# Layer 3 attention: work placed anew inside the steps of the memory chain, local attention in halves as full products, keys placed and values joined by GpSimd

## The reference, cut to what matters

```python
def step(carry, seg):
    mem, z = carry
    qq, kk, vv = seg
    sigma_q = jax.nn.elu(qq) + 1.0
    scores = jnp.einsum('bhsk,bhtk->bhst', qq, kk) / scale
    scores = jnp.where(causal_mask, scores, -jnp.inf)
    att_dot = jax.nn.softmax(scores, axis=-1) @ vv
    att_mem = sigma_q @ mem / (sigma_q @ z)
    sigma_k = jax.nn.elu(kk) + 1.0
    delta = vv - sigma_k @ mem / (sigma_k @ z)
    mem_new = mem + jnp.einsum('bhsk,bhsv->bhkv', sigma_k, delta)
    z_new = z + sigma_k.sum(axis=-2, keepdims=True).transpose(0, 1, 3, 2)
    att = beta * att_mem + (1.0 - beta) * att_dot
    out = att.reshape(Bsz, SEG, H * DV) @ Wo
    return ((mem_new, z_new), out)
```

## Time and profile before

| | |
|---|---|
| median of 3 runs | 1845.53 us (1842.15 to 1848.94) |
| span of the profiled execution | 1830.4 us |
| TensorE busy, of the span | 1617.1 us (88%) |
| VectorE busy | 984.5 us (54%) |
| ScalarE busy | 820.3 us (45%) |
| GpSimd busy | 355.9 us (19%) |

### The profile page before, as it was taken

How to read it: one execution, slowest core, us unless ns; L and a number is a source line. 1 busy time by engine, 2 the same in 40 slices (tenths; PEclk the granted TensorE clock), 3 DMA queues, 4 the chain that set the end, 5 groups by cost and what they waited for, 6 DMA issues and landing times. The chain is left out here.

```text
span 1830.4 us, 28085 instructions
## 1 busy us (share of the span) xinstructions
PE 1617.1 (88%) x9357; PEld 1274.0 (70%) x9358; DVE 984.5 (54%) x2336; ACT 820.3 (45%) x1798; POOL 355.9 (19%) x372
## 2 busy tenths in 40 slices
PE   4999996997639999787979989989999999999897
PEld 3778654875528888665637767867888888888655
DVE  2367346344555544224474445576676667666476
ACT  3577253333325555105755433364455445544344
POOL 2400020211066666573002121220000000000000
PEclk9999986998759999768989989999999999999899
DMA  3000030142615555332001042220000000000200
GB/s 121 12 18 1 1 147 9 43 105 59 255 60 168 168 170 168 107 104 78 1 0 38 32 117 77 72 81 1 18 17 17 0 17 17 17 0 0 46 0 23
DMA packets 55628, 109.35 MB, mean 60 GB/s; under 512 B 9905, under 2 KB 37425, under 8 KB 53914
## 3 DMA queue, kind: packets, MB, share of 16 engines
q1 hardware_dynamic: 45330, 82.10, 14.0%
q0 software_dynamic: 9168, 25.05, 4.8%
q10 hardware_dynamic: 1040, 1.05, 0.2%
HBM read 89.39 MB, written 18.78 MB: 59 GB/s over the span
## 5 line engine op out<-in xcount | busy, mean ns | idle before, releaser
L2776 ACT ACTIVATE l_mem<-bank 128x129 f32<-128x129 f32 x240 | 64.8, 279 | 185.6 <-PE bank L2630 184.7
L1681 POOL DMA_INDIRECT h_modulated<-l1f_rows,ln_rstd x127 | 120.5, 949 | 77.4 <-PE bank L1748 71.1
L1761 PE MATMUL bank<-l1f_up,l1f_wt 128*128 x508 | 104.4, 329 | 0.0
L2630 PE MATMUL bank<-l_dr,l_nkt 128*128 128x129 f32 x480 | 99.1, 309 | 2.9 <-DVE l_dr L2934 2.0
L3069 POOL MEMSET l3f_imp<- 96x2048 f32 x1 | 1.8, 1807 | 507.2 <-POOLq L88 507.2
L2931 DVE RECIPROCAL l_inv<-bank 128x1 f32<-128x1 f32 x240 | 38.9, 162 | 109.8 <-PE bank L2640 109.0
L2640 PE MATMUL bank<-l_mem,l_sg 128*128 128x129 f32 x480 | 84.4, 294 | 6.0 <-ACT l_mem L2776 0.2
L2934 DVE SCALAR_TENSOR_TENSOR l_dr<-bank,l_inv,l_v 128x128 f32<-128x128 f32 x240 | 84.3, 351 | 8.5
L1775 PE MATMUL bank<-l1f_down,ln_rstd 96*128 x254 | 87.5, 426 | 0.1
L2630 PEld LDWEIGHTS bank<-l_dr,l_nkt 128*128 128x128 f32 x480 | 68.5, 189 | 23.6 <-DVE l_dr L2934 19.4
L1804 PE MATMUL bank<-l1f_wt,ln_square 128*128 128x128 f32 x256 | 68.8, 426 | 18.2 <-DMA ln_square<-l1f_y_rows,l1f_back_at 16.9
(11 more groups left out here) (610 smaller groups left out, 4373.6 us busy)
## 6 DMA issues: line engine op xcount, KB each, us to landing
l1f_y_rows<-h_modulated SPq DMA_DIRECT2D x127, 128.0 KB
l1f_up<-in_l1f_up SPq DMA_DIRECT2D x8, 1536.0 KB
l_w<-in_l_w SPq DMA_DIRECT2D x9, 768.0 KB, 4.2
wmod<-in_wmod SPq DMA_DIRECT2D x4, 1536.0 KB, 10.1
l1f_down<-in_l1f_down SPq DMA_DIRECT2D x4, 1536.0 KB, 21.9
l2e_w<-in_l2f_win SPq DMA_DIRECT2D x14, 256.0 KB, 2.7
l_w<-in_l_wqk SPq DMA_DIRECT2D x8, 256.0 KB, 2.7
l0m_w<-in_l0f_win SPq DMA_DIRECT2D x8, 256.0 KB, 2.7
```

Of the source, the lines that this page charges most:

```text
L1681: pool.indirect_dma_start(xg[:, i % GETS], None, table, bass.IndirectOffsetOnAxis(ap=listing[:, i:i + 1], axis=0)).then_inc(got[i % GETS], 16)
L1761: last = pe.matmul(k.bank[:, UP + i % 2, 0:2 * F], xt[:, i % 2, b], up[:, bass.ds(owner_reg[i], 1), b, :], start=(b == 0), stop=(b == DB - 1))
L2630: pe.matmul(k.bank[:, MEM + a, 0:W1], nkt[:, a, n // 2, n % 2, :], dr[:, a, n, 0:W1], start=False, stop=False, skip_group_check=True).then ...
L2776: act.activation(mem[:, a, (n + 1) % 2, 0:W1], k.bank[:, MEM + a, 0:W1], ACT.Identity).then_inc(s["mem_copied"], 1)
```

## The change

Only `l3_attention` is changed.

1. GpSimd places the keys (`place_keys`), four copies of 128 x 512 a pair, instead of ScalarE. It also joins the values: `vj` has all 128 rows of each tile and head, made by two copies of 64 rows x 2048 elements a pair.
2. Local attention is 8 products of 128 rows and 128 columns a head (`vj` with the whole turned probabilities, whose off-diagonal blocks are zero), in two groups of four in two steps, each waiting for one of the two copies of the probabilities, which ScalarE now makes in two successive steps. `dot_scale` works on these halves.
3. `turn_reads` uses `pe.transpose` in the place of a product for tiles 0 to 6, in steps 14 (head 0) and 15 (head 1), without waits on the deltas; the last tile keeps its product (`turn_last_reads`).
4. The work in a step has three places: before the writes, between the write of head 0 and that of head 1, and after both. The output projection has 5 products in steps 1 to 4 and 4 in steps 5 to 7 (the last two one each in the second and third place).
5. Pieces of VectorE and ScalarE move to other steps accordingly.

```diff
+    OUT_PARTS = (0, 5, 10, 15, 20, 24, 28, 32)
+        vj = sb("vj", [P, TT, HP, P])
 ... on GpSimd:
+                def place_keys(i, a, c):
+                    if a or c:
+                        pool.wait_ge(s["keys_placed"], i * 4 + 2 * a + c)
+                    pool.wait_ge(s["sigma_ready"], i * 8 + 4 * a + c + 1)
+                    pool.tensor_copy(sg[:, a, 4 * c:4 * c + 4, 0::3, :], by_segment(keys[:, a, chunk(c)])
+                                     ).then_inc(s["keys_placed"], 1)
+                for i in range(PAIRS):
...
+                    for a in range(HP):
+                        for c in range(NCH):
+                            place_keys(i, a, c)
+                    pool.wait_ge(s["keys_placed"], i * 4 + 4)
+                    pool.wait_ge(s["v_even_copied"], i * 2 + 2)
+                    pool.tensor_copy(vj[EVEN], v[EVEN, :, :, 0, :]).then_inc(s["v_joined"], 1)
+                    pool.wait_ge(s["v_odd_copied"], i * 2 + 2)
+                    pool.wait_ge(s["v_joined"], i * 2 + 1)
+                    pool.tensor_copy(vj[ODD], v[ODD, :, :, 1, :]).then_inc(s["v_joined"], 1)
 ... on TensorE, turn_reads:
-                            last = pe.matmul(k.bank[:, 2 * a + o, t * S:(t + 1) * S], dr[half, a, 2 * t + o, 0:P],
-                                             turn[half, half], start=True, stop=True)
+                            last = pe.transpose(k.bank[:, 2 * a + o, t * S:(t + 1) * S], dr[half, a, 2 * t + o, 0:P],
+                                                turn[half, half])
 ... read_memory:
+                        if n == NS - 1 and not a:
+                            pe.wait_ge(s["dot_scaled"], i * 4 + 4)
 ... local_attention:
-                        for t in range(TT):
-                            for o, half in enumerate(HALF):
-                                last = pe.matmul(k.bank[:, 2 + o, t * S:(t + 1) * S], v[half, t, a, o, :],
-                                                 pt[half, a, t, half], start=True, stop=True)
+                        if begin % 4 == 0:
+                            pe.wait_ge(s["pt_copied"], i * 4 + (2 * a + c + 1))
...
+                        for t in range(begin, end):
+                            last = pe.matmul(k.bank[:, 2 + c, (t % 4) * P:(t % 4 + 1) * P], vj[:, t, a, :],
+                                             pt[:, a, t, :], start=True, stop=True)
 ... the places in a step:
+                    def before_writes(n):
+                        if n <= 7 and not first:
+                            project_out(i, OUT_PARTS[n - 1], OUT_PARTS[n] - 2)
+                        if n in (8, 11):
+                            turn_probs((n - 8) // 3, 0, 4)
+                        if n in (9, 10):
+                            local_attention(0, 4 * (n - 9), 4 * (n - 9) + 3)
+                        if n in (12, 13):
+                            local_attention(1, 4 * (n - 12), 4 * (n - 12) + 3)
                         if n == 14:
+                            turn_reads(i, 0, 0, LAST)
+                        if n == 15:
+                            turn_reads(i, 1, 0, LAST)
+                    def between_writes(n):
+                        if n <= 7 and not first:
+                            project_out(i, OUT_PARTS[n] - 2, OUT_PARTS[n] - 1)
+                        if n in (8, 11):
+                            turn_probs((n - 8) // 3, 4, 6)
+                        if n in (9, 10):
+                            local_attention(0, 4 * (n - 9) + 3, 4 * (n - 9) + 4)
+                        if n in (12, 13):
+                            local_attention(1, 4 * (n - 12) + 3, 4 * (n - 12) + 4)
+                    def after_writes(n):
+                        if n <= 7 and not first:
+                            project_out(i, OUT_PARTS[n] - 1, OUT_PARTS[n])
+                        if n in (8, 11):
+                            turn_probs((n - 8) // 3, 6, 8)
...
                         if n < NS - 1:
-                            for a in range(HP):
-                                write_memory(n, a)
-                            after_write(n)
+                            write_memory(n, 0)
+                            between_writes(n)
+                            write_memory(n, 1)
+                            after_writes(n)
 ... on ScalarE, behind the memory copies of step n:
-                        if n in (7, 9):
-                            for c in range(NCH):
-                                probs_copy((n - 7) // 2, c)
-                        if n in (8, 11):
-                            dot_scale((n - 8) // 3)
+                        if n in (8, 9):
+                            probs_copy(0, n - 8)
+                        if n in (11, 12):
+                            probs_copy(1, n - 11)
+                        if n in (9, 10):
+                            dot_scale(0, n - 9)
+                        if n in (12, 13):
+                            dot_scale(1, n - 12)
```

More of the change, by code:

```diff
@@ L2554, in turn_reads, with turn_last_reads @@
                 def turn_reads(i, a, begin, end):
-                    if begin == 0:
-                        for o in range(2):
-                            pe.wait_ge(s["dot_scaled" if a else "pt_copied"], i * 4 + (2 + o + 1))
-                    if begin == LAST:
-                        pe.wait_ge(s["reads_added"], i * 8 + (2 * a + 2))
                     for t in range(begin, end):
-                        pe.wait_ge(s["delta_ready"], i * CHAIN + (HP * 2 * t + a + 1))
                         for o, half in enumerate((ODD, EVEN)):
-                            last = pe.matmul(k.bank[:, 2 * a + o, t * S:(t + 1) * S], dr[half, a, 2 * t + o, 0:P],
-                                             turn[half, half], start=True, stop=True)
-                    if end >= LAST:
+                            last = pe.transpose(k.bank[:, 2 * a + o, t * S:(t + 1) * S], dr[half, a, 2 * t + o, 0:P],
+                                                turn[half, half])
+                    if end == LAST:
                         last.then_inc(s["turned"], 1)
+                def turn_last_reads(i, a):
+                    pe.wait_ge(s["reads_added"], i * 8 + (2 * a + 2))
+                    pe.wait_ge(s["delta_ready"], i * CHAIN + (HP * 2 * LAST + a + 1))
+                    for o, half in enumerate((ODD, EVEN)):
+                        last = pe.matmul(k.bank[:, 2 * a + o, LAST * S:TT * S], dr[half, a, 2 * LAST + o, 0:P],
+                                         turn[half, half], start=True, stop=True)
+                    last.then_inc(s["turned"], 1)
                 def pair(i, first):
@@ L2689, in after_write, with local_attention @@
-                    def after_write(n):
-                        if n <= 6 and not first:
-                            project_out(i, 5 * n - 2, 5 * n)
-                        if n == 7:
-                            turn_probs(0, 1)
-                        if n == 9:
-                            turn_probs(1, 1)
+                        if end % 4 == 0:
+                            last.then_inc(s["pt_ready"], 1)
+                    def local_attention(a, begin, end):
+                        c = begin // 4
+                        if begin % 4 == 0:
+                            pe.wait_ge(s["pt_copied"], i * 4 + (2 * a + c + 1))
+                            if a:
+                                pe.wait_ge(s["dot_scaled"], i * 4 + (c + 1))
+                        if begin == 0 and a == 0:
+                            pe.wait_ge(s["v_joined"], i * 2 + 2)
+                            if not first:
+                                pe.wait_ge(s["x_added"], i)
+                        for t in range(begin, end):
+                            last = pe.matmul(k.bank[:, 2 + c, (t % 4) * P:(t % 4 + 1) * P], vj[:, t, a, :],
+                                             pt[:, a, t, :], start=True, stop=True)
+                        if end % 4 == 0:
+                            last.then_inc(s["dot_ready"], 1)
```

97 lines of the change are left out of this document (33 added, 64 removed).

## The result

The changed kernel takes 1810.8 us (median of four runs, 1808.8 to 1812.9) where the kernel before, timed beside it, takes 1845.3: a ratio of 0.982 (95% interval 0.980 to 0.984). It is 34.5 us faster; the forecast was 28 (1817, range 1801 to 1835).

The account below looks back on a forecast made before the run. A chain of read, reciprocal, delta, write and copy was taken as the bound. Steps save 5.6 us a pair, less 0.3 tail and 1.7 GpSimd hold: 3.6, 28 in all, from 1845.5 to 1817 us, range 1801 to 1835.

Parts of the forecast that it names:

- The bound: Each pair's memory chain: read, reciprocal, delta, write, copy sets the time; TensorE's other work costs what it puts before a write.
- steps 2 to 14: Memory-chain steps of a pair after the first, forecast at 2.05, 2.2, 2.3 or 2.47 us each.
- Four full products at 2.47: Steps 9, 10, 12, 13: products wait for one copy of turned probabilities, so each step takes 2.47 us.
- Rival C: Copies of turned probabilities come late on ScalarE; the four steps with products stay near 3.2 us; 1840 us, chance 0.08.
- Local attention "no cheaper" as full products: TensorE's local attention: 8 full products or 32 half records both take 1.78 us a head.
- Turns: Turns of the reads as half-height transposes: 14 records a head at 0.056 us, 0.78 us; bounds 0.056 and 0.109.
- rival B: Half-height transposes on TensorE go at 0.109 us a record; 12 us more, 1829 us, chance 0.15.
- Tail: Between copy 14 and the next pair's projections, head 1's turns come in: 0.3 us a pair lost, bounds 0 and 0.8.
- The hold: GpSimd's placements and joins delay VectorE's SBUF-only sigma and capping before the first reciprocal: 1.7 us a pair, bounds 0 and 6.9.
- rival A: One-operand GpSimd copies hold nothing up on VectorE; 8 x 1.7 us back, 1804 us, chance 0.18.
- Rival D: Joins of 4.51 us hold VectorE between sigma 5 and the first delta; 42 us more, 1859 us, chance 0.06.
- Pair 0: Pair without output products, first steps at 2.07 us already: saves 0.6 us less; no granted clock below 1.00 expected.

## Why the prediction was right, point by point

The periods, each from a kernel that differs from another in one part, give the worth of each part:

| kernel | period, us |
|---|---|
| before | 61.28 |
| transposes in the old order | 59.82 |
| new order alone (halves, turns as products) | 59.85 |
| + transposes | 57.61 |
| + keys placed by GpSimd | 57.61 |
| + joins and full products, nothing held | 55.70 |
| as changed, joins early | 56.68 |

- **The bound.** Right: a chain of short waits, in which TensorE's other work costs what it puts ahead of a write. From this the forecast of steps 2 to 14 came out to 0.06 us, step 14's by two errors (see the turns). With nothing held the 14 steps take 30.98, against 31.1 forecast.
- **Four full products at 2.47.** Right, and for the reason given: with the copy a step earlier they take 2.20. Rival C (3.2 a step) is out with it.
- **Local attention "no cheaper" as full products.** True of the streaming time by which it was said, false of the kernel: halves in these places cost 1.91 us a pair more. The sum was not hurt, since it was worked out for full products. What it left out is the passage into and out of the 64-row form.
- **Turns.** Mis-sized: 0.029 a record, under the lower bound of 0.056 that I set, so rival B (0.109) is out. The step came out right (2.31) because a second term was missing: the turns begin 1.20 after copy 13, not 1.01, and then take 0.58 to the write, not 0.78. One error covered the other. (The sizes fit the passage into the 64-row form, but no run parts it from the rest of the 0.19.)
- **Tail.** 0.3 forecast, 0.15 measured (24.58 before, 24.73 after, from copy 14 to the next copy 0). The short transposes have a part in that: with the turns as products the tail is 25.86.
- **The hold.** The mechanism is right in each part: sigma held, capping held, deltas free, joins at 1.9; rival A is out. The term is mis-sized: 1.7 forecast, 0.98 measured. I let sigma 6 wait for the second placement and the first join begin behind sigma 6. Sigma 6 did wait (it lasts 0.88 and ends 0.54 after the placement), but that placement ended 0.4 earlier in the pair than worked out, and the join began 0.06 behind it, beside sigma 6. So the odd join ends 0.7 earlier in the pair. That the capping is held as well was right: it lasts 0.61 instead of 0.43 and ends 0.29 after the join. The Trainium skill, "SBUF — State Buffer", section "SBUF: two separate sides", has an operation in a two-port mode in the lock, and this trace agrees. Rival D, joins of 4.5 us, is out: they take 1.9 and 2.2. A single longer copy was not tried; a second copy behind the first costs nothing.
- **Pair 0.** Wrong. The prediction expected no granted clock below 1.00 in the layer, from a row of pair 2 alone. Held for a microsecond in step 1, in the one pair without output products, TensorE was then at 0.50 for 17 us, and the pair lost 4.0 (35.85 against 31.81 with idle products).

The sum a pair: 3.6 forecast, 4.60 measured; 0.7 of the difference is the hold, some 0.15 the tail, 0.1 the steps. Seven pairs give 32.2; pair 0's period is 0.6 longer in the profiled execution (60.03 to 60.65) instead of 3 shorter. That makes 31.6, near the 32.0 of the layer. So the total is in part luck: the over-priced hold (5 us in seven pairs) and the fall of the clock in pair 0 (4 us), which no term had, pull against each other. The other 2.5 us up to the medians' 34.5 is within what runs of one kernel differ by.

## What to carry to other kernels

In a chain of short waits price each step by what stands between a read and its write, and count for half-height work the passage into that form and back, not its streaming alone. Before giving GpSimd a copy, look which VectorE operations with operands in SBUF will be under way then: here one more wait, which starts the joins after the last of them, was worth 12 us, 4 of them through the clock of pair 0. After a change that lets a stage wait, look at the granted clock of its sparsest pass.

## What the runs showed of the hardware that I had not expected

- A stall of 1 us in a sparse stretch was followed by a granted clock of 0.50 for 17 to 20.5 us, in all three kernels that had it unfilled (one profile each); with 18 idle products it stayed at 1.00.
- Between two GpSimd copies, 0.06 to 0.13 us apart in the queue, the VectorE operation that waits goes first, so a GpSimd queue without a gap delays VectorE by one copy at a time.
- Of two VectorE operations with one SBUF operand of 128x512 the capping (0.43) was held by a GpSimd copy, the reduction (0.67, at 1361.47 above, beside L2565) was not. The Trainium skill, "VectorE: DVE Perf Modes", section "The perf-mode tier table (the rule you actually need)", has f32 `tensor_scalar` at double rate and `tensor_reduce` at single rate, which these two durations agree with; and by "SBUF — State Buffer", section "SBUF: two separate sides", also of the Trainium skill, an operation in a two-port mode takes part in the lock.
- Half-height transposes went at 0.029 us a record: the records of the two halves start in pairs, 0.005 us apart or less, a pair each 0.06. The same turns as f32 products start in pairs as well, a pair each 0.11, and take two records for each.
